# Eight PSUM banks shared out anew in the first expert layer of a graph network with experts

## The chip, the cores and the metric

One core of a Trainium2 chip runs the whole program. The metric is the device time of one execution in microseconds, the median of several runs. The kernel is written by hand in an engine-level language: each engine has its own instruction stream, and all order between engines comes from semaphores.

## The reference

Four layers follow each other on 6250 nodes with 256 features, each added to its input: a graph attention layer over 100000 edges of 8 types, a layer of 32 small experts with one expert a node, a second graph attention layer, and a layer of 8 large experts with two experts a node. The change touches the second of them:

```python
x = x + _L0_ffn_ref(_layernorm(x, axis=-1)[None], router_w, router_b, W1, b1, W2, b2)[0]
# in _L0_ffn_ref, E = 32 experts, D = 256, H = 64
logits = xf @ router_w.T + router_b
idx = jnp.argmax(logits, axis=-1)
h = relu(einsum('nd,ndh->nh', xf, W1[idx]) + b1[idx])
out = relu(einsum('nh,nhd->nd', h, W2[idx]) + b2[idx])
```

## The kernel before

`moe0` (L1374) is that layer. Its first part normalises the 49 tiles of 128 nodes, computes the logits, and sorts the nodes by expert into T = 80 tiles of 128 rows that each belong to one expert (4 more gathers stand at the end of the list and only feed the look-ahead). Its second part, a loop over these tiles in groups of four, is where the change lies. A full group of four is called a round below. For tile n the work is:

- GpSimd gathers the tile's 128 rows from the table of normalised rows, one indirect DMA a tile, into one of 8 slots (L1437). It waits until the slot's last tile has been turned.
- TensorE turns the rows, two 128x128 transposes (`turn`, L1649 to L1655), into 256 columns of a PSUM bank.
- ScalarE copies them out as the high fp16 half (`columns`, L1498 to L1500). VectorE subtracts that from the same PSUM columns and writes the low fp16 half (`column_rest`, L1595 to L1597).
- TensorE makes the inner rows, W1 of the tile's expert times the turned rows, three passes (high by high, high by low, low by high) of two matmuls, 64x128 out (L1660 to L1667).
- ScalarE adds the expert's b1 and applies relu, into `hT` (L1505 to L1507).
- TensorE makes the result, `hT` times W2 of the expert in fp32, 128x256 out (L1671 to L1675). Each appears as two matmul rows in the trace.
- VectorE adds b2 (L1604 to L1607), ScalarE applies relu (L1510 to L1512), and SyncE stores the tile (L1464 to L1466).

The order on each engine is written out by hand. TensorE does, in `four` (L1657): four tiles' inner rows, the turns of the next four, then the four results. ScalarE: four hidden rows, four columns of the next round, four relus. VectorE: four rests of the next round, then four additions. Each engine loads the numbers of the round's experts into registers at its top (`registers`, L282, used in L1504, L1601 and L1659).

A `Count` (L63) is a semaphore that starts at the number of places. `done(eng, t)` waits until tile t is finished. `slot(eng, t)` waits until tile t minus the number of places is finished, which is 4 for `h_ok` and `y_add`.

The eight PSUM banks are paired by tile: tile u of the round has its inner rows in bank 2u, and bank 2u + 1 holds its result in the first 256 columns and the turned rows of the next round in the last 256. Since TensorE may not write a bank while another engine reads it, the result matmul waits, besides for its hidden rows, until VectorE has read the turned rows of the tile in the same bank (L1674), and the turns wait until the additions that read the bank are done (L1669).

Of the kernel before, what the change touches and what calls it, by code (L numbers as in the profile page):

```python
# [8 lines left out]
ALU = mybir.AluOpType  # L9
ACT = mybir.ActivationFunctionType  # L10
AX = mybir.AxisListType

P = 128
N = 6250
D = 256
# [7 lines left out]
E0, F0 = 32, 64  # L23
# [109 lines left out]
def col(ap, start, size=1):  # L133

    out = ap[:, start:start + size] if isinstance(start, int) else ap[:, bass.ds(start, size)]
    if size == 1 and len(ap.shape) > 2:
        names = " ".join("abcd"[: len(ap.shape) - 2])
        out = out.rearrange(f"p o {names} -> p (o {names})")
    return out
# [1234 lines left out]
def moe0(nc, a, k):  # L1374

    with Stage(nc, "moe0") as s:
        bank = s.banks()
# [8 lines left out]
        w1_in, w1 = s.sb("w1_rows", [P, DC, E0, F0]), [s.sb(f"w1_{n}", [P, DC, E0, F0], F16) for n in ("high", "low")]  # L1386
# [13 lines left out]
        xn, xnT = space[:, 0:XN, :], space[:, XN:XN + 2, :]  # L1400
        rw_n, rw = s.sb("router_natural", [E0, D]), s.sb("router", [P, DC, E0])
        rb = s.sb("router_bias", [P, E0])
        w2 = s.sb("w2", [F0, E0, D])
        b1_n, b1, b2 = s.sb("b1_rows", [E0, F0]), s.sb("b1_T", [F0, E0]), s.sb("b2", [P, E0, D])
        x = b2[:, 0:AHEAD * CH, :].rearrange("p (n t) f -> p n t f", n=AHEAD)
# [64 lines left out]
        @block.scalar  # L1470
        def _(act):
            act.dma_start(rw_n[:, :], a["L0_ffn_router_w"]).then_inc(router, 16)
            act.dma_start(rb[:, :], a["L0_ffn_router_b"].rearrange("(o e) -> o e", o=1).broadcast_to([P, E0])).then_inc(router, 16)
            act.dma_start(b1_n[:, :], a["L0_ffn_b1"]).then_inc(router, 16)
            def load_piece(i):
                c, e0 = i % DC, i // DC * EQ
                act.dma_start(w1_in[:, c, e0:e0 + EQ, :], a["L0_ffn_W1"][e0:e0 + EQ, c * P:(c + 1) * P, :].rearrange("e p h -> p e h")).then_inc(loaded, 16)
            for c in range(CHUNKS):
                part = slice(c * CH, (c + 1) * CH)
                act.wait_ge(var_ok, c + 1)  # L1480
                nc.scalar.activation(sd[:, part], var[:, part], ACT.Sqrt).then_inc(sd_ok, 1)
                for t in range(c * CH, (c + 1) * CH):
                    if t >= CH and t % 2 and (t - CH) // 2 < PIECES0:
                        load_piece((t - CH) // 2)
                    if t >= NT - 4:
                        q, h = divmod(t - NT + 4, 2)
                        act.wait_ge(loaded, PIECES0 * 16)
                        nc.scalar.activation(w1[0][:, q, h * E0 // 2:(h + 1) * E0 // 2, :], w1_in[:, q, h * E0 // 2:(h + 1) * E0 // 2, :], ACT.Copy, scale=WS).then_inc(w1_hi, 1)
                    act.wait_ge(t_ps, t + 1)
                    if t >= 2:  # L1490
                        act.wait_ge(lg_ps, t - 1)
                    nc.scalar.activation(xnT[:, t % 2, :], bank[t % 2][:, 0:D], ACT.Copy).then_inc(t_ok, 1)
            route.slot_lanes(act)
            act.wait_ge(route_ok, 1)
            for n in (x_hi, h_ok, y_ok):
                n.start(act)

            def columns(t, u):  # L1498
                x_ps.done(act, t)
                nc.scalar.activation(xT[0][:, u, :], bank[2 * u + 1][:, D:2 * D], ACT.Copy, scale=XS).then_inc(x_hi.sem, 1)  # L1500
            for u in range(4):
                columns(u, u)
            with act.Fori(0, T // 4) as i:
                e = registers(nc, mybir.EngineType.Activation, route.expert[0:1, bass.ds(i * 4, 4)], E0 - 1)  # L1504
                for u in range(4):  # L1505
                    h_ps.done(act, i * 4 + u)
                    nc.scalar.activation(hT[:, u, :], bank[2 * u][0:F0, 0:P], ACT.Relu, bias=col(b1, e[u]), scale=1.0 / (XS * WS)).then_inc(h_ok.sem, 1)  # L1507
                for u in range(4):
                    columns(i * 4 + 4 + u, u)
                for u in range(4):  # L1510
                    y_add.done(act, i * 4 + u)
                    nc.scalar.activation(y[:, u, :], y[:, u, :], ACT.Relu).then_inc(y_ok.sem, 1)  # L1512

        @block.vector
        def _(v):
# [78 lines left out]

            def column_rest(t, u):  # L1595
                x_hi.done(v, t)
                nc.vector.scalar_tensor_tensor(xT[1][:, u, :], bank[2 * u + 1][:, D:2 * D], XS, xT[0][:, u, :], ALU.mult, ALU.subtract).then_inc(x_ok.sem, 1)  # L1597
            for u in range(4):
                column_rest(u, u)
            with v.Fori(0, T // 4) as i:  # L1600
                e = registers(nc, mybir.EngineType.DVE, route.expert[0:1, bass.ds(i * 4, 4)], E0 - 1)  # L1601
                for u in range(4):
                    column_rest(i * 4 + 4 + u, u)
                for u in range(4):  # L1604
                    y_ps.done(v, i * 4 + u)
                    out_ok.slot(v, i, u)
                    nc.vector.tensor_tensor(y[:, u, :], bank[2 * u + 1][:, 0:D], col(b2, e[u]), ALU.add).then_inc(y_add.sem, 1)  # L1607

        @block.tensor
        def _(pe):  # L1610
# [38 lines left out]
            def turn(i, slot):  # L1649

                u = slot % 4
                pe.wait_ge(tile_in[slot], (i + 1) * 16)
                for c in range(DC):
                    last = nc.tensor.transpose(bank[2 * u + 1][:, D + c * P:D + (c + 1) * P], taken(slot)[:, c * P:(c + 1) * P], k.ident[:, :])
                last.then_inc(x_ps.sem, 1)  # L1655

            def four(n, i, half):  # L1657

                e = registers(nc, mybir.EngineType.PE, route.expert[0:1, bass.ds(n, 4)], E0 - 1)  # L1659
                for u in range(4):  # L1660
                    x_ok.done(pe, n + u)
                    h_ok.slot(pe, n + u)
                    for part, (pw, px) in enumerate(passes):
                        for c in range(DC):
                            last = nc.tensor.matmul(bank[2 * u][0:F0, 0:P], col(w1[pw][:, c], e[u]), xT[px][:, u, c * P:(c + 1) * P],
                                                    start=(part == 0 and c == 0), stop=(part == 2 and c == DC - 1))
                    last.then_inc(h_ps.sem, 1)  # L1667
                for u in range(4):
                    y_add.slot(pe, n + u)  # L1669
                    turn(i + half, 4 * (1 - half) + u)  # L1670
                for u in range(4):  # L1671
                    h_ok.done(pe, n + u)

                    x_ok.done(pe, n + 4 + u)  # L1674
                    nc.tensor.matmul(bank[2 * u + 1][:, 0:D], hT[:, u, :], col(w2, e[u]), start=True, stop=True).then_inc(y_ps.sem, 1)  # L1675
            for u in range(4):
                turn(0, u)
            with pe.Fori(0, T // 8) as i:
# [825 lines left out]
```

## Time and profile before

| | us |
|---|---|
| median of 3 runs | 3104.38 (3100.57 to 3109.21) |
| profiled execution, its own time | 3113.99 |
| its span, first to last instruction | 3112.2 |
| mean granted TensorE clock, share of full | 0.781 |
| busy: TensorE matmul, DVE, ACT, GpSimd | 2071.2, 1808.6, 1376.4, 1563.4 |

The tile loop of the first expert layer runs from about 1889 to 2050 us of the span. PE is TensorE's matmul, PEld its weight loads, DVE VectorE, ACT ScalarE, POOL GpSimd. A group row gives starts or counts and busy time, then in brackets the idle time ahead of it and what ended that. In a timeline row, "x4" is four instructions of one line merged: the row's second number is the time from the first one's start to the last one's end. Ends of matmuls are modelled.

### The profile page before, as it was taken

What the parts mean: (1) busy time and instruction counts of PE and PEld (TensorE: products, weight loads), DVE (VectorE), ACT (ScalarE), POOL (GpSimd) and SP (SyncE); (2) the same over time, 40 slices, a digit from 0 to 9 for tenths busy, and PEclk for the clock granted to TensorE, in tenths of its full rate; (3) what the DMA queues carried; (4) which work ended last, traced back from release to release, by engine and by line L of the source; (5) the groups of instructions that cost most, each with busy time, mean ns of one, the idle gap of its engine ahead of it and who ended that gap; (6) DMA issues with size and microseconds to landing.
All of it is one profiled execution on the core that took longest, in us unless ns stands there. A gap on an engine that the chain in (4) does not pass through costs nothing. (4 is left out here: it accounts for less than half of the span.)

```text
span 3112.2 us, 48944 instructions
## 1 busy us (share of the span) xinstructions
PE 2071.2 (67%) x13115; PEld 1560.9 (50%) x13116; DVE 1808.6 (58%) x4427; ACT 1376.4 (44%) x3064; POOL 1563.4 (50%) x1492
## 2 busy tenths in 40 slices
PE   8999216665566555655656546856143599999998
PEld 5555104443344344433444444644032379999997
DVE  5423126565566565665666884445488686656565
ACT  4454125454455444545544124533044664444443
POOL 0066645666666666666662314443640145555554
PEclk9999557687777776777778556768555599999999
DMA  7576533444444444444441623565432162222331
GB/s 232 205 270 257 174 88 113 126 127 117 129 121 121 129 120 123 127 120 119 128 117 33 174 101 92 137 141 144 88 105 65 40 179 47 45 47 46 49 47 27
DMA packets 194692, 363.31 MB, mean 117 GB/s; under 512 B 52783, under 2 KB 127126, under 8 KB 187983
## 3 DMA queue, kind: packets, MB, share of 16 engines
q0 software_dynamic: 78160, 187.31, 25.0%
q1 hardware_dynamic: 106126, 171.10, 16.4%
q10 hardware_dynamic: 10240, 2.95, 0.4%
q8 instruction: 74, 1.21, 0.2%
q14 instruction: 92, 0.75, 0.1%
HBM read 246.22 MB, written 117.28 MB: 117 GB/s over the span
## 5 line engine op out<-in xcount | busy, mean ns | idle before, releaser
L834 POOL DMA_INDIRECT sum_ring<-h_tab,gnn_edge_row x880 | 838.1, 952 | 482.0 <-issue 244.8
L1107 PE MATMUL sum_bank<-sum_ring,sum_one_hot 128*128 128x264 f32 x1760 | 613.2, 494 | 218.0 <-DVE nodes_acc L971 110.8
L1107 PEld LDWEIGHTS sum_bank<-sum_ring,sum_one_hot 128*128 128x128 f32 x1760 | 397.3, 242 | 349.0 <-issue 275.7
L878 ACT ACTIVATE sum_one_hot_T<-sum_distance,sum_pick_unit 128x1024 f16<-128x1024 bf16 x110 | 126.3, 1148 | 619.5 <-remote 569.4
L2235 POOL DMA_INDIRECT out_dram<-moe_y,slots_nodes x112 | 193.4, 1726 | 262.0 <-ACT moe_y L2257 239.9
L964 DVE TENSOR_TENSOR sum_ring<-sum_ring,sum_bank 128x1024 f32<-128x1024 f32 x220 | 266.9, 1214 | 90.4 <-ACT sum_ring L906 85.3
L885 ACT ACTIVATE sum_distance_by_lane<-all_iota,gnn_minus_local 128x128 bf16<-128x128 f32 x880 | 267.4, 386 | 0.1
L2409 PE MATMUL moe_bank<-moe_w_high,slots_early 128*128 x896 | 245.7, 274 | 7.6 <-DVE moe_w_low L1737 7.6
L2409 PE MATMUL moe_bank<-moe_w_high,moe_hidden_low 128*128 x896 | 245.7, 274 | 0.0
L2409 PE MATMUL moe_bank<-moe_w_low,slots_early 128*128 x896 | 245.6, 274 | 0.0
L2226 POOL DMA_INDIRECT moe_tile<-normal,slots_rows x116 | 136.3, 1175 | 187.9 <-PEq L71 134.6
L971 DVE TENSOR_TENSOR nodes_acc<-sum_bank,nodes_acc 128x264 f32 x440 | 187.4, 426 | 39.5 <-remote 24.5
L1096 PE MATMUL sum_bank<-gnn_dst_half_high,sum_one_hot_T 128*128 x880 | 119.2, 215 | 135.8 <-issue 95.1
L2273 ACT ACTIVATE slots_early<-moe_bank,moe_b_T 128x256 f32<-128x256 f32 x456 | 184.6, 478 | 34.9 <-PE moe_bank L2399 19.3
L513 ACT ACTIVATE rows_h_rows<-rows_bank 128x436 f32<-128x436 f32 (+1 forms) x245 | 125.9, 523 | 146.4 <-PE rows_bank L752 126.0
L2399 PE MATMUL moe_bank<-moe_x_high,moe_w_high 128*128 128x256 f16 x912 | 174.5, 273 | 0.4 <-issue 0.4
L2399 PE MATMUL moe_bank<-moe_x_low,moe_w_high 128*128 128x256 f16 x912 | 174.5, 273 | 0.0
L2399 PE MATMUL moe_bank<-moe_x_high,moe_w_low 128*128 128x256 f16 x912 | 174.3, 273 | 0.0
L1096 PEld LDWEIGHTS sum_bank<-gnn_dst_half_high,sum_one_hot_T 128*128 128x128 f16 x880 | 88.3, 111 | 160.2 <-issue 151.7
L942 DVE TENSOR_TENSOR sum_kept_relation<-sum_bank,sum_relation 128x512 f32<-128x512 f32 x110 | 75.5, 686 | 155.4 <-remote 111.0
L2341 DVE SCALAR_TENSOR_TENSOR moe_hidden_low<-slots_early 128x512 f16<-128x512 f32 x228 | 158.3, 694 | 7.8
L752 PE MATMUL rows_bank<-rows_w_high,rows_xnT_high 128*128 128x436 f16 (+1 forms) x490 | 131.6, 350 | 4.6 <-DVE gnn_dst_half_low L626 4.6
(449 smaller groups left out, 4545.6 us busy)
## 6 DMA issues: line engine op xcount, KB each, us to landing
h_tab<-rows_h_rows SPq DMA_DIRECT2D x49, 1056.0 KB
sum_local_rows<-local_tab SPq DMA_DIRECT2D x110, 256.0 KB
slots_stage<-in_L_ffn_W_dram SPq DMA_DIRECT2D x14, 1024.0 KB
sum_ring<-h_tab,gnn_edge_row POOLq DMA_INDIRECT x880
mask_tab<-rows_masks POOLq DMA_DIRECT2D x7, 1560.0 KB
sum_masks<-mask_tab SPq DMA_DIRECT2D x28, 390.0 KB
results<-moe_tiles SPq DMA_DIRECT2D x80, 128.0 KB
g_tab<-gnn_rows_out SPq DMA_DIRECT2D x49, 132.0 KB
```

The lines of the kernel that those rows point to most:

```text
L834: nc.gpsimd.indirect_dma_start(ring[:, t % (RING * ST), :], None, k.h_tab, bass.IndirectOffsetOnAxis(k.edge_row[:, t:t + 1], 0)).then_inc( ...
L885: last = nc.scalar.activation(off[:, u * P:(u + 1) * P], k.iota[:, :], ACT.Abs, bias=k.minus_local[:, m * ST + u:m * ST + u + 1])
L964: nc.vector.tensor_tensor(to, to, by, ALU.mult).then_inc(msg_ok, 1)
L971: nc.vector.tensor_tensor(col(k.acc, b), sum_b[g % SG][:, 0:W0], col(k.acc, b), ALU.add).then_inc(added, 1)
L1096: last = nc.tensor.matmul(pick_b[n % 2][:, u * R * H0:(u + 1) * R * H0], hotT[:, n % 2, u, :], col(part_, b[u // G]), start=(j == 0), stop ...
L1107: last = nc.tensor.matmul(sum_b[j][:, 0:W0], hot[:, m % 3, t, :], ring[:, m % RING * ST + t, :], start=(u == 0), stop=(u == G - 1))
L2226: nc.gpsimd.indirect_dma_start(xi[:, n % 2, h, :], None, k.xn1, bass.IndirectOffsetOnAxis(k.slot_row[:, 2 * n + h:2 * n + h + 1], 0)).then ...
L2235: nc.gpsimd.indirect_dma_start(a["out"], bass.IndirectOffsetOnAxis(k.slot_node[:, 2 * n + h:2 * n + h + 1], 0), y[:, n % 2, h, :], None, b ...
L2273: last = nc.scalar.activation(hg[:, q, m * B1:(m + 1) * B1], bank[q][:, m * B1:(m + 1) * B1], ACT.Gelu, scale=1.0 / (XS * WS), bias=col(b1 ...
L2341: nc.vector.scalar_tensor_tensor(low, f, HS, high, ALU.mult, ALU.subtract).then_inc(hs_ok.sem, 1)
L2399: last = nc.tensor.matmul(bank[q][:, m * B1:(m + 1) * B1], w1[pw][:, c, bass.ds(e * F1 + (2 * q + m) * P, P)], xh[px][:, u, c, :], start=( ...
L2409: last = nc.tensor.matmul(bank[6 + u][:, h * D:(h + 1) * D], hh[ph][:, u, m, h * P:(h + 1) * P], col(w2[pw], e)[:, m * D:(m + 1) * D], sta ...
```

## The change

The turned rows get a bank of their own for each tile (0 to 3), the inner rows two banks in turn (4 and 5), the results two banks in turn (6 and 7). The inner product of tile n now waits until the hidden rows of tile n - 2 have been read out, and the result of tile n until the addition of tile n - 2 has read its bank. The wait of the turns on the additions and the wait of the results on the rests of the next round go.

```diff
+        x_bank, h_bank, y_bank = (lambda u: bank[u]), (lambda u: bank[4 + u % 2]), (lambda u: bank[6 + u % 2])
...
-                nc.scalar.activation(xT[0][:, u, :], bank[2 * u + 1][:, D:2 * D], ACT.Copy, scale=XS).then_inc(x_hi.sem, 1)
+                nc.scalar.activation(xT[0][:, u, :], x_bank(u)[:, 0:D], ACT.Copy, scale=XS).then_inc(x_hi.sem, 1)
...
-                    nc.scalar.activation(hT[:, u, :], bank[2 * u][0:F0, 0:P], ACT.Relu, bias=col(b1, e[u]), scale=1.0 / (XS * WS)).then_inc(h_ok.sem, 1)
+                    nc.scalar.activation(hT[:, u, :], h_bank(u)[0:F0, 0:P], ACT.Relu, bias=col(b1, e[u]), scale=1.0 / (XS * WS)).then_inc(h_ok.sem, 1)
...
-                nc.vector.scalar_tensor_tensor(xT[1][:, u, :], bank[2 * u + 1][:, D:2 * D], XS, xT[0][:, u, :], ALU.mult, ALU.subtract).then_inc(x_ok.sem, 1)
+                nc.vector.scalar_tensor_tensor(xT[1][:, u, :], x_bank(u)[:, 0:D], XS, xT[0][:, u, :], ALU.mult, ALU.subtract).then_inc(x_ok.sem, 1)
...
-                    nc.vector.tensor_tensor(y[:, u, :], bank[2 * u + 1][:, 0:D], col(b2, e[u]), ALU.add).then_inc(y_add.sem, 1)
+                    nc.vector.tensor_tensor(y[:, u, :], y_bank(u)[:, 0:D], col(b2, e[u]), ALU.add).then_inc(y_add.sem, 1)
...
-                    last = nc.tensor.transpose(bank[2 * u + 1][:, D + c * P:D + (c + 1) * P], taken(slot)[:, c * P:(c + 1) * P], k.ident[:, :])
+                    last = nc.tensor.transpose(x_bank(u)[:, c * P:(c + 1) * P], taken(slot)[:, c * P:(c + 1) * P], k.ident[:, :])
...
                     x_ok.done(pe, n + u)
-                    h_ok.slot(pe, n + u)
+                    h_ok.slot(pe, n + u + 2)
...
-                            last = nc.tensor.matmul(bank[2 * u][0:F0, 0:P], col(w1[pw][:, c], e[u]), xT[px][:, u, c * P:(c + 1) * P],
+                            last = nc.tensor.matmul(h_bank(u)[0:F0, 0:P], col(w1[pw][:, c], e[u]), xT[px][:, u, c * P:(c + 1) * P],
...
                 for u in range(4):
-                    y_add.slot(pe, n + u)
                     turn(i + half, 4 * (1 - half) + u)
                 for u in range(4):
                     h_ok.done(pe, n + u)
-
-                    x_ok.done(pe, n + 4 + u)
-                    nc.tensor.matmul(bank[2 * u + 1][:, 0:D], hT[:, u, :], col(w2, e[u]), start=True, stop=True).then_inc(y_ps.sem, 1)
+                    y_add.slot(pe, n + u + 2)
+                    nc.tensor.matmul(y_bank(u)[:, 0:D], hT[:, u, :], col(w2, e[u]), start=True, stop=True).then_inc(y_ps.sem, 1)
```

## Rows read from the trace of the kernel before

**Rows 1.** Busy time by stretch: loop's steady part, three rounds; PEclk is the clock.
```profile
core 0: us, PE busy (x) PEld busy (x) DVE busy (x) ACT busy (x) POOL busy (x), PEclk, DMA share, GB/s
1905.00:2033.00 128.00, 112.29 (x682) 85.87 (x682) 53.73 (x137) 69.70 (x204) 63.98 (x69) 0.77 0.56 138
1963.29:1969.83 6.54, 5.30 (x42) 3.92 (x41) 3.02 (x8) 3.27 (x11) 3.78 (x4) 1.00 0.52 133
1969.83:1977.45 7.62, 6.16 (x41) 4.58 (x41) 3.02 (x8) 4.64 (x15) 3.79 (x4) 0.81 0.55 165
1947.53:1955.83 8.30, 8.30 (x41) 6.59 (x40) 3.40 (x8) 4.60 (x13) 3.77 (x4) 0.50 0.51 151
```

**Rows 2.** Waits in the loop, 1886 to 2052: total us, times, longest.
```profile
POOL moe_tiles L1437 <- PE moe_bank L1654: 26.0, 14, 3.9
POOL moe_pick L1437 <- PE moe_bank L1654: 25.2, 12, 3.8
ACT moe_hidden_T L1507 <- PE moe_bank L1665: 24.2, 25, 3.6
...
PE moe_bank L1675 <- DVE moe_tiles L1597: 7.1, 6, 5.1
...
PE moe_bank L1675 <- issue: 4.9, 7, 0.9
```

**Rows 3.** Timeline of a full-clock round: start, us, engine, line, count, idle before.
```profile
1962.77 0.47 PE L1665 MATMUL moe_bank<-moe_tiles,moe_w_high 128*64 128x128 f16 x4 [0.87 <-issue]
...
1963.29 1.10 PE L1654 MATMUL moe_bank<-all_ident,moe_pick 128*128 128x128 f32 x8
1963.76 1.21 ACT L1500 ACTIVATE moe_tiles<-moe_bank 128x256 f16<-128x256 f32 x4
...
1964.18 1.42 DVE L1597 SCALAR_TENSOR_TENSOR moe_tiles<-moe_bank,moe_tiles 128x256 f16<-128x256 f32 x4 [3.97 <-ACT moe_tiles L1500]
1964.74 1.59 PEld L1675 LDWEIGHTS moe_bank<-moe_w,moe_hidden_T 64*128 64x128 f32 x8 [0.59 <-issue]
1964.75 1.99 PE L1675 MATMUL moe_bank<-moe_w,moe_hidden_T 64*128 x8 [0.36 <-DVE moe_tiles L1597]
...
1965.69 1.61 DVE L1607 TENSOR_TENSOR moe_tiles<-moe_bank,moe_b 128x256 f32<-128x256 f32 x4
1966.14 1.61 ACT L1512 ACTIVATE moe_tiles<-moe_tiles 128x256 f32<-128x256 f32 x4 [1.17 <-DVE moe_tiles L1607]
...
1966.66 0.41 PE L1665 MATMUL moe_bank<-moe_tiles,moe_w_high 128*64 128x128 f16 x4
...
1968.24 0.47 PE L1665 MATMUL moe_bank<-moe_tiles,moe_w_high 128*64 128x128 f16 x4
...
1969.83 1.09 PE L1654 MATMUL moe_bank<-all_ident,moe_tiles 128*128 128x128 f32 x8 [0.54 <-issue]
1969.86 1.12 ACT L1507 ACTIVATE moe_hidden_T<-moe_bank,moe_b_T 64x128 f32<-64x128 f32 x4 [2.11 <-PE moe_bank L1665]
```

**Rows 4.** Timeline of DVE, 1965.9 to 1966.1: additions 0 and 1 merged.
```profile
1965.69 0.76 DVE L1607 TENSOR_TENSOR moe_tiles<-moe_bank,moe_b 128x256 f32<-128x256 f32 x2
```

**Rows 5.** Line L284, the load of expert numbers, on TensorE's sequencer, 1960 to 1970.
```profile
L284 PEldq TENSOR_LOAD <-moe_expert x1: 333/333/333, 1965.9 to 1965.9; - x1
```

**Rows 6.** Timeline of a half-clock round, columns as in rows 3.
```profile
1949.43 3.78 PE L1675 MATMUL moe_bank<-moe_w,moe_hidden_T 64*128 x8
...
1950.89 0.42 DVE L1607 TENSOR_TENSOR moe_tiles<-moe_bank,moe_b 128x256 f32<-128x256 f32 x1 [0.52 <-PE moe_bank L1675]
...
1953.81 0.42 ACT L1512 ACTIVATE moe_tiles<-moe_tiles 128x256 f32<-128x256 f32 x1 [0.44 <-issue]
...
1954.41 0.63 PE L1665 MATMUL moe_bank<-moe_tiles,moe_w_high 128*64 128x128 f16 x4
1954.63 1.12 ACT L1507 ACTIVATE moe_hidden_T<-moe_bank,moe_b_T 64x128 f32<-64x128 f32 x3 [0.41 <-PE moe_bank L1665]
...
1956.03 0.36 ACT L1507 ACTIVATE moe_hidden_T<-moe_bank,moe_b_T 64x128 f32<-64x128 f32 x1 [0.28 <-PE moe_bank L1665]
```

## Prediction

> **What bounds the kernel now.** I read the busy time by stretch first, because the change touches one loop only, the first expert layer's 80 tiles in 20 groups of four; I call one group a round and count its tiles 0 to 3. Nothing of the next layer starts before this loop has ended, so time lost or won there goes one for one into the span. In the steady part TensorE is busy 112.29 of 128 us, DVE 53.73, ACT 69.70 and GpSimd 63.98 [rows 1]: TensorE is the nearest to full, and the granted clock averages 0.77. The single rounds under it show why it is an average: one at clock 1.00 takes 6.54 us from turn to turn with 5.30 us of matmul, the next, partly at the low level, 7.62, and one at 0.50 takes 8.30 us with matmul in all 8.30. So at half clock (1.2 GHz) TensorE is the bound, and at full clock (2.4 GHz) a chain of waits is. Then I read the waits: TensorE's idle time ahead of L1675, where the shared bank makes it wait, is 7.1 us for DVE's L1597 and 4.9 us of issue in the whole stage, and ACT waits 24.2 us for the inner rows of L1665 [rows 2]. GpSimd waits for TensorE, 26.0 and 25.2 us, so the gathers aren't the bound.
>
> Last the order of one full-clock round [rows 3]. Turns start at 1963.29, ACT's columns at 1963.76, DVE's rests at 1964.18; the result matmuls start at 1964.75, the additions at 1965.69, the last relu ends at 1967.75, and the inner products start at 1966.66. ACT's four hidden rows (L1507) come only at 1969.86, 2.11 us after its last relu, though the first inner product is shown ending near 1967.2. At half clock the same step of ACT takes 0.40 us (relu ends 1954.23, hidden row at 1954.63) [rows 6]. So in full-clock rounds some 1.7 us pass in which the release of the inner rows is late; no row says why.
>
> **The change, part by part.** No instruction of work is added or removed; addresses and waits differ.
>
> Removed: TensorE's wait for DVE's rest of the next tile ahead of each result matmul (L1674). It ends a gap of 0.36 us in the round read [rows 3], 12.0 us over the stage at most [rows 2]. The wait on the additions ahead of the turns (L1669) was met long before (additions end at 1967.30, the next turns start at 1969.83): nothing.
>
> Added first: result 2 waits for addition 0, result 3 for addition 1. DVE's program puts all four rests ahead of addition 0, so this doesn't come earlier: addition 0 runs 1965.69 to 1966.11 and addition 1 ends at 1966.45 [rows 3, 4]. A wait that ends reaches the array 0.14 us later (rest 0 ends 1964.60, weights at 1964.74). Result 2 then starts at 1966.25. Eight result matmuls take 1.99 us, so four take about 1.15, and results end at 1967.40 instead of 1966.74: **+0.66 us** for the last addition and relu, which now end at 1968.41. The 0.36 us won at result 0 are lost in this, since results 0 and 1 only finish earlier and stand still. Behind the wait on TensorE's queue stands the load of the next four experts' numbers, now at 1965.9 beside the result matmuls [rows 5]. Inner products start 1.06 us after the last wait (rest 3 ends 1965.60, start 1966.66), so now at 1967.5. That 0.85 us isn't added to the rest, because of the next wait.
>
> Added second: inner product 2 waits for ACT's hidden row 0, and 3 for row 1. Behind it on TensorE are the turns, and who waits for those are ACT, DVE and GpSimd's gathers. If the release is on time, ACT gets to hidden row 0 0.40 us after relu, at 1968.81, takes 0.36 [rows 6], and inner product 2 starts at 1969.31. Product 3 follows by one tile's pitch, (1968.24 - 1966.66) / 3 = 0.53, and the turns 0.52 after it (1962.77 to 1963.29): 1970.36, a round of **7.07 us**. Without the wait the same arithmetic gives 1968.24 + 0.52 = 1968.76, 5.47 us, and the trace shows 6.54 and 7.62, mean 7.08, with the late release.
>
> So a full-clock round has three readings. The late release is in the timed runs of before and goes with the new pause: 7.07 against 7.08, 0.0. It stays in both: 7.07 + 1.7, **+1.7**. It belongs to the recording and is in no timed run: 7.07 against 5.47, **+1.6**. No row shows TensorE pausing between two inner products with a release outstanding, so I take 1.1, nearer to the two that agree, and keep 0.0 and 1.7.
>
> Half-clock rounds: inner product 2 would start at 1954.41; hidden row 0 ends at 1954.63 + 0.36 = 1954.99, plus 0.14: +0.7 us [rows 6]. The result wait costs a little too: addition 0 starts at 1950.89, when result 0 is there, and ends at 1951.31, so result 2 could start at 1951.45; undelayed it would start about half way through the 3.78 us that begin at 1949.43, some 1.85 us in, at 1951.28: **+0.2**, and the relus and hidden row 0 are later by as much. A half-clock round costs **+0.9 us**.
>
> How many: 0.77 is 46% of the time at half level. Of 20 rounds the last has none behind it. Of the other 19, 8 at 8.30 and 11 at 7.08 give 66.4 of 144.3 us at half clock, which is 46%: I take 8 and 11. GpSimd has eight slots and 3.8 us of work in a round, SP's stores follow the relu: both move along, nothing is added.
>
> The sum is 11 x 1.1 + 8 x 0.9 = 12.1 + 7.2 = **+19 us**, with ends 11 x 0 + 7.2 = +7 and 11 x 1.7 + 7.2 = +26. Against the profiled execution (span 3112.2, its own time 3113.99) that is 3133. That execution stands 9.6 us over the median of the runs, 3104.38, which I use: **3123 us**.
>
> Here a rule speaks against the change: the Trainium skill, in Perfetto Trace Analysis, Matmul Optimizations, wants all eight PSUM banks in use so that most instructions can be in flight. Both kernels use eight, but the inner rows drop from four to two; the rows agree in that the pause above is just what the two missing banks cost.
>
> **The rivals.**
> *Covered pause* (the other side, not slower by what can be told): the 1.7 us of late release before inner rows are where the new wait falls, and the pause lets the release come on time. Place: ACT's L1507; price: 0.0 per full-clock round plus at most the 7.2 us, 3104 to 3112 us. It decides if hidden row 0 starts within 0.5 us of the last relu. For it: the release always comes after TensorE's issue gaps late in the inner products. Against: the pause comes at the same place in every round, and the excess of the profiled execution hints that part of the lateness is recording.
>
> *The clock goes down too.* The round at 1.00 has matmul in 5.30 of its 6.54 us, and the round after it already averages 0.81 [rows 1]; with 7.1 to 8.8 us for the same matmuls there is more idle time still. If six of the 11 rounds fell to half clock, each would take 8.30 + 0.9 = 9.2 in place of 7.08 + 1.1 = 8.2: +6 on the sum, 3129 us. If all fell: 11 x (9.2 - 7.08) + 7.2 = +31, 3135 us. Against: at half clock matmul fills the round, and the clock comes back. The Trainium skill's TensorE: Matmul & The Clock Gate, HAM oscillation, has the same: idle TensorE falls to the half rate, and the next work starts at it; the rows agree, with 0.50 and 1.00 inside one stage.
>
> *The shared bank was the cost* (faster): all 12.0 us ahead of the result matmuls go and the new waits are met in time. It decides at addition 0: it would have to end before result 1, at about 1965.3, and ends at 1966.11, since DVE does the rests first. It gives -12.0 + 7.2 = -5; with the half-clock part gone as well -12, which is 3092 to 3099 us. The Trainium skill's PSUM — Partial Sum Buffer, on bank collisions, is the rule behind it: guard by bank and not by address, so that own banks need no guard between rests and results.
>
> That the change doesn't do what it says isn't likely: the three bank functions name eight different banks, and each has its wait.
>
> **How the numbers follow.** What a measurement of this kernel can tell from no change is about 0.3%, 9.3 us. The forecast (+9.3 to +26, 3114 to 3130) gets 0.55, the clock rival 0.15, the covered pause 0.22, the shared bank 0.08. Slower is the first two, 0.70; same 0.22; faster 0.08. The range takes in the whole covered pause, from 3104, and the clock rival at its top, 3135, with the 4 us by which runs of before lie off their median: 3104 to 3140.
>
> **What would show it.** Right: in full-clock rounds a gap on TensorE of 0.5 us or more ahead of the third inner product, ended by ACT's L1507; one ahead of the third result matmul, ended by DVE's L1607; none ended by L1597; L1507 in two pairs rather than four in a row; a turn-to-turn time of 7.1 us or more at full clock and 9.2 at half. Wrong: hidden row 0 starting within 0.5 us of relu while rounds stay at 7.1, which is the covered pause; rounds below 6.5 us, which is the shared bank; a mean clock below 0.7 in the stage, which is the clock rival.

## The result and the profile after

The changed kernel's median is 3141.97 us (3133.09 to 3145.71, 4 runs) against 3106.8 us (3100.57 to 3110.1, 4 runs) for the kernel before, run beside it: **ratio 1.0096, 95% interval 1.0075 to 1.0118**. Slower, by about 30 us of 3107. The ratio on record is not the quotient of the two medians, which is 1.0113, or 35 us; I go by the ratio. It was measured a second time (after_again, below): 1.0107, interval 1.0085 to 1.013. Of the versions below, one run of own (4867.52 us) and one of after_act (4213.99 us) lie far above all others and are in no ratio.

I read the profiled execution in the same order as before. First the busy time by stretch. These are the head of the page of the changed kernel and its granted clock in 40 slices:

```profile
span 3137.0 us, 48924 instructions
...
PE 2103.7 (67%) x13115; PEld 1577.8 (50%) x13116; DVE 1808.4 (58%) x4427; ACT 1386.4 (44%) x3064; POOL 1564.3 (50%) x1492
...
PEclk9999558777787677877688555559555599999999
```

The same lines of the kernel before:

```profile
span 3112.2 us, 48944 instructions
...
PE 2071.2 (67%) x13115; PEld 1560.9 (50%) x13116; DVE 1808.6 (58%) x4427; ACT 1376.4 (44%) x3064; POOL 1563.4 (50%) x1492
...
PEclk9999557687777776777778556768555599999999
```

The number of matmuls is the same, 13115, and TensorE is busy 32.5 us longer with them. DVE and GpSimd do the same work in the same time. Nothing was added, so the matmuls themselves ran slower: the clock. In the slices (some 78 us each) the loop lies in the 25th to 27th: 555 after, 676 before. The windows tell it exactly. Busy time by stretch, kernel after (columns as in rows 1): the whole loop from the first turn to the end of the last relu, two rounds that follow each other, and the stretches behind the loop:

```profile
1886.00:2083.10 197.10, 173.89 (x808) 122.14 (x808) 68.49 (x164) 91.83 (x244) 77.22 (x82) 0.54 0.42 107
1936.15:1945.78 9.63, 8.95 (x41) 6.28 (x40) 3.39 (x8) 4.54 (x12) 3.77 (x4) 0.50 0.35 109
...
1945.78:1954.14 8.36, 7.20 (x41) 5.38 (x40) 3.20 (x8) 4.51 (x12) 3.77 (x4) 0.70 0.40 106
...
2083.10:2286.00 202.90, 81.99 (x354) 63.99 (x354) 101.41 (x331) 45.58 (x125) 108.97 (x112) 0.68 0.51 124
```

and the kernel before:

```profile
1889.30:2048.50 159.20, 132.61 (x808) 100.33 (x808) 64.46 (x164) 82.95 (x244) 77.11 (x82) 0.76 0.54 131
...
2048.50:2260.00 211.50, 83.33 (x354) 64.64 (x354) 101.51 (x330) 45.09 (x125) 111.26 (x115) 0.67 0.50 122
```

The loop takes 197.1 us in place of 159.2, **+37.9 us**, with the same 808 matmuls, and the mean granted clock falls from 0.76 to 0.54. There is no round at the full level in this execution. Of the 18 rounds that follow the fill of the pipe, 13 take 9.60 to 9.63 us at 0.50 (the row at 1936.15 is one), four 8.32 to 8.39 us at about 0.70 (the row at 1945.78) and one 8.95 us; in the kernel before they take 5.49 to 8.31 us (three of them in [rows 1]), 7.38 on average against 9.30 now. That is 18 x 1.92 = 34.6 us; the other 3.3 us are at the two ends of the loop.

The spans differ by 24.8 us only. The stretch ahead of the loop was 3.3 us shorter in this execution (1886.0 against 1889.3), and the time behind the loop 9.8 us shorter (3137.0 - 2083.1 = 1053.9 against 3112.2 - 2048.5 = 1063.7), most of it in the stretch next to the loop, 202.9 against 211.5 us for the same 354 matmuls. The change doesn't touch either. Behind the loop it is the profiled execution of the kernel before that stands out, with its 1063.7 us: in the two executions of the changed kernel and the eight of the versions below that leave the stages behind the loop alone this time is 1047.8 to 1057.8 us, and its whole time was 9.6 us over its median as well. So the two spans understate the change, and the ratio of the timed runs (+30 us) stands between span and loop. From here on I compare loops.

Second the waits. Waits of TensorE in the loop, 1886 to 2084, kernel after (total us, times, longest):

```profile
PE moe_bank L1655 <- DMA moe_tiles<-normal,moe_slot_rows: 12.4, 4, 10.8
PE moe_bank L1666 <- ACT moe_hidden_T L1508: 8.9, 15, 1.2
PE moe_bank L1674 <- DVE moe_tiles L1608: 5.0, 6, 2.5
PE moe_bank L1666 <- issue: 4.8, 7, 2.5
```

The wait on DVE's rests that stood here before (L1597, 7.1 us) [rows 2] is gone. In its place are the two new ones, 8.9 us ahead of the inner products (L1666) for ACT's hidden rows (L1508) and 5.0 us ahead of the results (L1674) for DVE's additions (L1608). The first row is the fill of the pipe at the start, 10.8 us in one piece. In the second execution the two waits are 11.2 and 6.4 us. The 8.9 us is no large number against 37.9: the waits give the place, not the price.

Third a half-clock round of the kernel after, the timeline (columns as in rows 3):

```profile
1936.15 1.97 PE L1655 MATMUL moe_bank<-all_ident,moe_pick 128*128 128x128 f32 x8
...
1938.05 4.21 PE L1674 MATMUL moe_bank<-moe_w,moe_hidden_T 64*128 x8
...
1939.52 0.42 DVE L1608 TENSOR_TENSOR moe_tiles<-moe_bank,moe_b 128x256 f32<-128x256 f32 x1 [0.52 <-PE moe_bank L1674]
...
1940.18 0.50 PEld L1674 LDWEIGHTS moe_bank<-moe_w,moe_hidden_T 64*128 64x128 f32 x2 [0.78 <-issue]
...
1942.19 0.63 PE L1666 MATMUL moe_bank<-moe_tiles,moe_w_high 128*64 128x128 f16 x4
...
1942.83 0.63 PE L1666 MATMUL moe_bank<-moe_tiles,moe_w_high 128*64 128x128 f16 x4
1942.86 0.42 ACT L1513 ACTIVATE moe_tiles<-moe_tiles 128x256 f32<-128x256 f32 x1 [0.44 <-DVE moe_tiles L1608]
...
1943.68 0.62 ACT L1508 ACTIVATE moe_hidden_T<-moe_bank,moe_b_T 64x128 f32<-64x128 f32 x2 [0.41 <-PE moe_bank L1666]
...
1944.29 0.64 PE L1666 MATMUL moe_bank<-moe_tiles,moe_w_high 128*64 128x128 f16 x4 [0.62 <-ACT moe_hidden_T L1508]
...
1945.78 1.54 PE L1655 MATMUL moe_bank<-all_ident,moe_tiles 128*128 128x128 f32 x6
```

The reader is to see two things. The eight result matmuls take 4.21 us, where they took 3.78 [rows 6]: result 2 waits for addition 0, which starts at 1939.52 and ends at 1939.94, and the weights come at 1940.18. And the third inner product, which would follow the second by its pitch of 0.64 us at 1942.83 + 0.64 = 1943.47, starts at 1944.29, because ACT's hidden row 0 starts at 1943.68, 0.41 us after its last relu. That is +0.43 and +0.82 us; the rest of the +1.33 us (9.63 - 8.30), 0.08 us, lies between the third product and the turns.

### The profile page after: what moved, and what is told of

The parts are those of the page before. It is cut to its first block and busy times, and to the rows that moved or that the text cites. A ratio compares the mean times of both kernels' runs of the same rounds, so it can differ in the third digit from the quotient of the medians.

```text
span 3137.0 us, 48924 instructions
## 1 busy us (share of the span) xinstructions
PE 2103.7 (67%) x13115; PEld 1577.8 (50%) x13116; DVE 1808.4 (58%) x4427; ACT 1386.4 (44%) x3064; POOL 1564.3 (50%) x1492
## 3 DMA queue, kind: packets, MB, share of 16 engines
q0 software_dynamic: 78160, 187.31, 24.8%
## 5 line engine op out<-in xcount | busy, mean ns | idle before, releaser
L977 DVE TENSOR_SCALAR sum_under_max<-sum_bank 128x256 f32<-128x256 f32 x28 | 11.9, 424 | 214.0 <-remote 213.3
```

## The experiments

Loop times are from the first turn to the end of the last relu in one profiled execution of each; two executions of the changed kernel have 197.1 and 192.6 us, so a few us are scatter. Ratios are those on record, to the kernel before run beside each; where they are set against each other, remember their intervals of some 0.002 to each side (6 us). The granted clock is that of the loop.

| kernel | ratio (95%) | loop, us | clock |
|---|---|---|---|
| before | 1 | 159.2 | 0.76 |
| after | 1.0096 (1.0075 to 1.0118) | 197.1 | 0.54 |
| after_again | 1.0107 (1.0085 to 1.013) | 192.6 | 0.58 |
| own | 0.9977 (0.9961 to 0.9994) | 149.2 | 0.80 |
| h2 | 1.0068 (1.0042 to 1.0095) | 180.0 | 0.67 |
| y2 | 1.0016 (0.9996 to 1.0036) | 164.0 | 0.79 |
| fill | 1.005 (1.0032 to 1.0068) | 171.5 | 0.87 |
| before_fill | 0.9989 (0.9979 to 1.0) | 157.3 | 0.84 |
| own_fill | 0.9981 (0.9968 to 0.9994) | 146.0 | 0.91 |
| after_act | 1.0084 (1.0061 to 1.0107) | 181.6 | 0.65 |
| after_both | 1.0082 (1.0066 to 1.0099) | 182.2 | 0.66 |
| nostore | 1.0117 (1.0088 to 1.0145), stores behind the loop | 161.1 | 0.73 |

Own, h2, y2 and fill ran on one chip; the other fills and orders on a second, and on that one nostore and after_again later, together.

### own: no wait between tiles u and u + 2

The turned rows keep a bank each. The inner row and the result of one tile share a bank, in different columns: the result of tile n is written only when its hidden row has been read, so their lives don't overlap.

```diff
-        x_bank, h_bank, y_bank = (lambda u: bank[u]), (lambda u: bank[4 + u % 2]), (lambda u: bank[6 + u % 2])
+        x_bank, h_bank, y_bank = (lambda u: bank[u]), (lambda u: bank[4 + u]), (lambda u: bank[4 + u][:, D:2 * D])
...
-                    h_ok.slot(pe, n + u + 2)
+                    y_add.slot(pe, n + u)
...
-                    y_add.slot(pe, n + u + 2)
```

> Turned rows in banks 0 to 3 as in the change, but inner rows and result of a tile share bank 4 + u, so that neither new wait stands: the result matmul waits for its own hidden rows alone, the inner product for the addition of tile n - 4. Theory (the two new waits cost the time, directly and through the clock): no loss against the kernel before, a loop of 135 us or less between the first result and the last, ratio 0.990 to 1.000. Rival (it is the new place of the turned rows, or some effect of bank addresses): as slow as the changed kernel, ratio about 1.010.

Measured: 3079.82 us against 3085.31, ratio 0.9977 (0.9961 to 0.9994), the loop 149.2 us; from the first result to the last it is 138.0 us, a little over the 135 expected. The loop and a full-clock round of own in the windows:

```profile
1870.80:2020.00 149.20, 127.67 (x808) 96.43 (x808) 60.85 (x164) 79.57 (x244) 77.13 (x82) 0.80 0.59 140
...
1903.58:1909.51 5.93, 5.31 (x41) 3.96 (x41) 2.74 (x8) 3.60 (x12) 3.78 (x4) 1.00 0.54 161
...
1943.08:1951.39 8.31, 8.31 (x42) 6.60 (x41) 3.37 (x8) 4.92 (x14) 3.78 (x4) 0.50 0.54 162
```

The half-clock round is back at 8.31 us, with matmul in all of it, as in the kernel before [rows 1]. Own is 7 us faster than the kernel before by the ratio, 10 by the loop. That is most likely the removed wait on the rests, though own also gives inner row and result one bank, and no run takes the two apart. What costs in the change is the two banks in turn, not the new places of the turned rows. This version beats both kernels, the kernel before by a little. Its late release is still there: in the round about 1897 of own ACT stands

```profile
1897.25 1.12 ACT L1508 ACTIVATE moe_hidden_T<-moe_bank,moe_b_T 64x128 f32<-64x128 f32 x4 [2.17 <-PE moe_bank L1666]
```

2.17 us ahead of its four hidden rows. No inner product waits for them here; the first to read them are the results, behind the turns, and what these wait is small over the whole loop:

```profile
PE moe_bank L1673 <- ACT moe_hidden_T L1508: 3.3, 5, 2.1
```

### h2 and y2: each of the two pairs by itself

h2 is the kernel before with the inner rows in two banks in turn:

```diff
-                    nc.scalar.activation(hT[:, u, :], bank[2 * u][0:F0, 0:P], ACT.Relu, bias=col(b1, e[u]), scale=1.0 / (XS * WS)).then_inc(h_ok.sem, 1)
+                    nc.scalar.activation(hT[:, u, :], bank[2 * (u % 2)][0:F0, 0:P], ACT.Relu, bias=col(b1, e[u]), scale=1.0 / (XS * WS)).then_inc(h_ok.sem, 1)
...
-                    h_ok.slot(pe, n + u)
+                    h_ok.slot(pe, n + u + 2)
...
-                            last = nc.tensor.matmul(bank[2 * u][0:F0, 0:P], col(w1[pw][:, c], e[u]), xT[px][:, u, c * P:(c + 1) * P],
+                            last = nc.tensor.matmul(bank[2 * (u % 2)][0:F0, 0:P], col(w1[pw][:, c], e[u]), xT[px][:, u, c * P:(c + 1) * P],
```

> The kernel before with the inner rows alone moved to two banks in turn, so that only the wait of an inner product for the hidden row of tile n - 2 is added. Theory (this wait is the larger one, +0.7 of the +0.9 us in a half-clock round, and it is enough to keep the clock low): rounds of about 9 us, ratio 1.006 to 1.010, mean clock of the loop below 0.65. Rival (the wait of the results is the one that matters): ratio below 1.004 and a loop clock near the 0.77 of before.

y2 is own with the results in two banks in turn:

```diff
-        x_bank, h_bank, y_bank = (lambda u: bank[u]), (lambda u: bank[4 + u]), (lambda u: bank[4 + u][:, D:2 * D])
+        x_bank, h_bank, y_bank = (lambda u: bank[u]), (lambda u: bank[4 + u]), (lambda u: bank[6 + u % 2][:, D:2 * D])
...
+                    if u < 2:
+                        h_ok.done(pe, n + u + 2)
+                    y_add.slot(pe, n + u + 2)
```

Since its results lie in the banks of inner rows 2 and 3, results 0 and 1 wait for those hidden rows too. That binds once, while the pipe fills (5.1 us, with the first two rounds 1.7 us longer than in own), and in no steady round.

> Turned rows in banks 0 to 3, inner rows in banks 4 to 7, results in two banks in turn (columns 256 to 511 of banks 6 and 7), so that only the wait of a result for the addition of tile n - 2 binds. Theory (the hidden-row wait is the larger part): full-clock rounds longer by up to 0.8 us, half-clock rounds by 0.2, ratio 1.001 to 1.005. Rival (this wait is what lowers the clock): ratio 1.008 or more, loop clock below 0.65.

Measured: h2 1.0068 (3111.13 against 3085.31 us), loop 180.0 us; y2 1.0016 (3091.44), loop 164.0. Busy time of the loop of h2, and its wait rows:

```profile
1882.10:2062.10 180.00, 146.41 (x808) 110.40 (x808) 66.64 (x164) 89.02 (x244) 77.50 (x82) 0.67 0.47 116
```

```profile
PE moe_bank L1665 <- ACT moe_hidden_T L1507: 14.1, 18, 2.5
```

The wait for hidden rows alone is seen 18 times and costs 180.0 - 159.2 = 20.8 us of loop, 21 us by the ratio; the half-clock round is 9.15 to 9.18 us, +0.9. The clock, 0.67, did not fall below the 0.65 expected. In y2 the wait stands ahead of the third result, here in a full-clock round:

```profile
1909.05 1.09 PE L1655 MATMUL moe_bank<-all_ident,moe_tiles 128*128 128x128 f32 x8
...
1911.93 1.12 PE L1676 MATMUL moe_bank<-moe_w,moe_hidden_T 64*128 x4 [0.74 <-DVE moe_tiles L1608]
```

The wait costs 164.0 - 149.2 = 14.8 us of loop against own, and (1.0016 - 0.9977) x 3085 = 12 us by the ratios. The prediction left out the later start of the inner products (0.85 us), as covered by the wait for hidden rows. Alone the result wait is worth 0.4 us in a half-clock round (8.73 against 8.31) and brings full-clock rounds to 7.0 to 7.3 us. Both together, after against own, are 47.9 us of loop (43.4 with the second execution), 12.3 (7.8) more than the sum of the two. By the ratios the two add up to 0.0107 and both together are 0.0119 (0.0130 with after_again), a difference within the intervals: that they cost more together than apart is seen in the profiled loops and not shown by the timed runs. The clock goes the same way as the loops: 0.80 (own), 0.79 (y2), 0.67 (h2), 0.54 (both).

### fill, before_fill, own_fill: the same waits at another clock

Ten small matmuls, whose result nobody reads, are put into the pause ahead of the third inner product, where TensorE would otherwise stand still:

```diff
+                    if u == 2:
+                        for _ in range(10):
+                            nc.tensor.matmul(bank[0][0:F0, D:D + P], w1[0][:, 0, 0, :], xT[0][:, 0, 0:P], start=True, stop=True)
```

fill adds them to the changed kernel, own_fill to own; in before_fill they go to the idle columns of bank 1, behind a wait for the addition that last read it.

> The changed kernel with ten extra 64x128 matmuls into unused columns of bank 0 between the second and the third inner product of a round, work that the reference doesn't have and nothing reads. At full clock they take about 0.6 us, at half clock 1.1 us, in the place of the new wait. Theory (idle time in the wait keeps the clock at half): the clock rises in more of the loop, above 0.65 from 0.55, and the kernel is no slower than the changed one or up to 15 us faster. Rival (the waits cost time by themselves and the clock follows from something else): clock stays at 0.55, and the kernel is as slow or slower by up to 20 x 0.3 = 6 us.

> The kernel before with the same ten extra matmuls, into unused columns of bank 1, between the second and the third inner product; nothing reads them. At full clock they add about 0.6 us to a round, at half clock 1.1. Theory (the clock follows how busy TensorE is kept, and half-clock rounds are the dear ones): the loop's mean clock rises from 0.77 to above 0.85, and the loop's time stays within 5 us of the 159 us before in spite of 200 more matmuls. Rival (the clock doesn't follow them): clock 0.77, the loop longer by 19 x 0.6 to 19 x 1.1 = 11 to 21 us.

> The kernel without either wait (turned rows in banks 0 to 3, inner rows and result of a tile in bank 4 + u) with the ten extra matmuls into bank 0. Loop so far 149.3 us at a clock of 0.81. Theory of the clock: nearly all rounds at full clock, mean above 0.88, rounds of 6.5 to 7.3 us, so the loop at 140 to 150 us and the kernel level with the one without them. Rival: clock stays at 0.81, the loop 11 to 20 us longer.

The loop of fill, and one of its rounds:

```profile
1872.80:2044.30 171.50, 136.35 (x1008) 101.61 (x1008) 60.30 (x164) 84.22 (x244) 77.18 (x82) 0.87 0.50 123
...
1951.47:1959.18 7.71, 6.10 (x52) 4.42 (x51) 2.93 (x8) 4.13 (x12) 3.79 (x4) 1.00 0.53 142
```

With 200 matmuls more than the changed kernel (1008 against 808) the loop is 25.6 us **shorter** (171.5 against 197.1), TensorE's busy time 37.5 us shorter (136.35 against 173.89), and the clock is 0.87 in place of 0.54. The ratio goes from 1.0096 to 1.005, the intervals apart. So with the clock come back 25.6 of 37.9 us by the loops, and 0.0046 of 0.0096, 14 of 30 us, by the ratios; the other 171.5 - 159.2 = 12.3 us of loop stay. The round of fill shows the longer chain of waits at full clock:

```profile
1954.35 1.12 PE L1677 MATMUL moe_bank<-moe_w,moe_hidden_T 64*128 x4 [0.74 <-DVE moe_tiles L1608]
...
1956.60 0.72 PE L1664 MATMUL moe_bank<-moe_tiles,moe_w_high 128*64 128x128 f16 x10
...
1957.08 0.36 ACT L1508 ACTIVATE moe_hidden_T<-moe_bank,moe_b_T 64x128 f32<-64x128 f32 x1 [0.58 <-issue]
...
1957.68 0.47 PE L1669 MATMUL moe_bank<-moe_tiles,moe_w_high 128*64 128x128 f16 x4 [0.36 <-ACT moe_hidden_T L1508]
...
1958.66 0.47 PE L1669 MATMUL moe_bank<-moe_tiles,moe_w_high 128*64 128x128 f16 x4 [0.40 <-ACT moe_hidden_T L1508]
```

The ten (0.72 us, L1664) lie in the pause; it is still not filled, 0.36 us are left, and the fourth product has a wait of its own, 0.40 us.

On the others the same ten do little: before_fill 0.9989 with 157.3 us, clock 0.84 (just under the 0.85 expected); own_fill 0.9981 with 146.0 us, clock 0.91, against own's 0.9977 and 149.2 us. The loop of before_fill:

```profile
1874.50:2031.80 157.30, 128.00 (x1008) 102.28 (x1008) 62.41 (x164) 80.80 (x244) 77.47 (x82) 0.84 0.57 134
```

In own_fill 13 of the 18 rounds are at 1.00 and still take 5.4 to 7.6 us: there a chain of waits bounds the round, and a higher clock has little left to give.

The pair fill and before_fill also gives a fairer price of the waits, since both have the ten: 1.0050 - 0.9989 = 0.0061, 19 us, or 171.5 - 157.3 = 14.2 us of loop. Of the loss without them that leaves 11 us by the ratios and 23.7 us by the loops to what goes with the low clock. So the clock's part is a third to a half by the timed runs and over 60% by the profiled loops; the rest is the two waits themselves. A reading that fits is that the changed kernel's clock stays down because its rounds at half clock have a pause in them as well. That the small matmuls raise the clock is shown by the three; that nothing else of them works is not.

### after_act and after_both: another order on ACT and DVE

If the price is that ACT does all four relus ahead of hidden row 0, hidden rows first should take it away. after_act:

```diff
                 for u in range(4):
+                    if u == 1 and not first:
+                        for w in (2, 3):
+                            relu(i * 4 - 4 + w, w)
...
-                for u in range(4):
-                    y_add.done(act, i * 4 + u)
-                    nc.scalar.activation(y[:, u, :], y[:, u, :], ACT.Relu).then_inc(y_ok.sem, 1)
+                for u in range(2):
+                    relu(i * 4 + u, u)
```

(the lines of the first loop follow the hidden row of u; the first round is peeled, and the last two relus stand behind the loop). after_both has DVE's additions between the rests as well:

```diff
-                for u in range(4):
-                    column_rest(i * 4 + 4 + u, u)
-                for u in range(4):
+                for op, u in ((0, 0), (0, 1), (1, 0), (0, 2), (1, 1), (0, 3), (1, 2), (1, 3)):
+                    if op == 0:
+                        column_rest(i * 4 + 4 + u, u)
+                        continue
```

> The changed kernel with ScalarE's order altered: hidden rows 0 and 1 of a round come ahead of relus 2 and 3 of the round before. Banks and waits are those of the change. Theory (the third inner product waits because ScalarE's hidden row 0 stands behind the last relu and the register load): the gap ahead of the third inner product shrinks from 0.62 us to 0.1 or less, the kernel comes to where the results' wait alone stands, ratio 1.001 to 1.004 instead of 1.010. Rival (the two banks are too few whatever ScalarE's order): ratio 1.008 or more.

> As the last, and VectorE's order altered too: rest 0, rest 1, addition 0, rest 2, addition 1, rest 3, additions 2 and 3, so that result 2 doesn't wait for all four rests. Theory: both new waits nearly vanish with the banks of the change kept; ratio 0.996 to 1.001, loop 150 to 160 us. Rival (the rests are now late for the next inner products, or the banks themselves cost): ratio 1.004 or more.

Both miss, and the rivals' ratios, 1.008 or more and 1.004 or more, are met. The ratios are 1.0084 and 1.0082 (26 and 25 us), within the interval of the changed kernel; the loops, 181.6 and 182.2 us, are 22 and 23 us over the kernel before, and shorter than the 197.1 and 192.6 us of the changed kernel's two executions. So the order buys back a part at most, and no part that the timed runs can show. Here is the round of after_both at the higher clock:

```profile
1958.29 1.35 PE L1686 MATMUL moe_bank<-moe_w,moe_hidden_T 64*128 x4 [0.49 <-DVE moe_tiles L1620]
...
1962.24 0.36 ACT L1512 ACTIVATE moe_hidden_T<-moe_bank,moe_b_T 64x128 f32<-64x128 f32 x1 [1.40 <-PE moe_bank L1678]
...
1962.85 0.65 PE L1678 MATMUL moe_bank<-moe_tiles,moe_w_high 128*64 128x128 f16 x4 [1.12 <-ACT moe_hidden_T L1512]
```

The fourth product waits for hidden row 1, which ACT starts at 1962.24, after 1.40 us idle, though the records of its inner product (the second) end at 1961.04. That is the late release of the prediction. In own little waits for it (3.3 us in all); with two banks in turn TensorE itself waits for it, 1.12 us here. At half clock the order helps (rounds of 9.2 instead of 9.6 us). So an earlier place for the hidden rows buys back 0.4 us in some rounds, and is exposed to the release in others.

### nostore: is the late release the stores'?

In the kernel before, the loop's stores of the results are left out and 80 stores of the same size come after the loop; so the rows that are stored are not the layer's, and its time outside the loop is not to be compared.

```diff
-                sp.dma_start(rows(k.ys0, (i * 4 + u) * P, P), y[:, u, :]).then_inc(out_ok.sems[u], 16)
+                sp.sem_inc(out_ok.sems[u], 16)
...
+            for t in range(T):
+                sp.dma_start(rows(k.ys0, t * P, P), y[:, t % 4, :]).then_inc(late_st, 16)
+            sp.wait_ge(late_st, T * 16)
```

> The kernel before with SyncE's 80 stores of result tiles taken out of the loop (the semaphore is counted up in their place) and issued after it, so that the rows stored are the last four tiles' and not the layer's; some 60 us of stores stand behind the loop. It asks where ScalarE's late hidden rows of full-clock rounds come from (2.1 us after the last relu instead of 0.4). Theory A (SyncE's store issues hold up TensorE's releases): the gap falls to about 0.4 to 0.6 us in all rounds and full-clock rounds take 5.5 to 6.5 us. Theory B (it comes from the dense inner products alone): the gap stays near 2 us in full-clock rounds.

Measured: a loop of 161.1 us against 159.2, with half the traffic:

```profile
1881.50:2042.60 161.10, 136.88 (x808) 103.62 (x808) 65.07 (x164) 84.85 (x244) 77.23 (x82) 0.73 0.33 68
```

68 GB/s instead of 131, and nothing gained. Three of its rounds still have ACT stand 2.07 to 2.16 us between relu and hidden row; others above half clock have mostly 0.66 to 1.58 us. One of each:

```profile
1925.87 1.18 ACT L1511 ACTIVATE moe_hidden_T<-moe_bank,moe_b_T 64x128 f32<-64x128 f32 x4 [2.09 <-PE moe_bank L1669]
...
1931.63 0.36 ACT L1511 ACTIVATE moe_hidden_T<-moe_bank,moe_b_T 64x128 f32<-64x128 f32 x1 [0.68 <-PE moe_bank L1669]
```

The stores don't bound the loop. They may have a part in the lateness: in the four rounds at 0.97 to 1.00 the first hidden row comes 0.66 to 1.34 us after the last relu, where such rounds of the kernel before have 1.68 to 2.12 us in all but the last, but the second hidden row then waits another 0.53 to 1.27 us. They aren't the only cause. What the cause is stays open.

### after_again

The changed kernel once more, no edit, beside nostore.

> The changed kernel once more, beside the same runs of the kernel before as the others of this set. Theory: a ratio of 1.008 to 1.012, the loop at 190 to 198 us and its clock near 0.55. Rival (the low clock of the first profile was one execution's chance): clock above 0.65 and a loop below 185 us.

Measured: 3137.51 against 3104.54 us, 1.0107 (1.0085 to 1.013). The loop takes 192.6 us at 0.58, with rounds of 9.63 us at 0.50 in 12 of the 18; two rounds are at 0.90 and 0.91 and take 7.79 and 8.25 us. The low clock is the kernel's, not one execution's.

## Why the prediction was right, and where it was not

**The side** was right, and by its mechanism: the wait of inner product 2 on ACT's hidden row 0. Undoing the two pairs (own) takes the whole loss away, and h2 alone gives 21 us of it. But it is not the whole mechanism: the rival *the clock goes down too*, which also makes the kernel slower and had got 0.15, is at work beside it. **The number** is short. Forecast 3123 us, +19; measured 3141.97 us, which is 2 us above the upper end of the range, 3140. Part of that is the kernel before, whose median rose from 3104.38 to 3106.8 us; by the ratio, 3104.38 x 1.0096 = 3134 us, +30, the time of the rival *the clock goes down too*, all rounds (3135 us). Step by step:

- **Removed wait (taken at nothing).** The row of L1597 is gone, but it was most likely worth more than nothing: own, without it and without the waits on tile n - 2, gains 7 us. With the result wait added the gain is gone, as forecast (y2, 1.0016).
- **Result wait at full clock (+0.66 us).** Placed right. In fill result 2 starts 2.88 us after the turns (1954.35 - 1951.47), forecast 1966.25 - 1963.29 = 2.96.
- **Inner product 2 at full clock.** Forecast 6.02 us after the turns (1969.31 - 1963.29), in fill 6.21 (1957.68 - 1951.47). The failed piece is "Product 3 follows by one tile's pitch": it was put 0.53 us behind product 2 and stands 0.98 behind it, since its own wait for hidden row 1 (0.40 us) is a second link. So the round is 7.71 us and not 7.07.
- **The three readings.** The first one's premise holds in the profiled executions: the pause takes the place of the late release. In fill ACT's gap ahead of hidden row 0 is 0.58 us, and in the changed kernel 0.40 to 0.61 us in 17 of the 18 rounds, against up to 2.17 us before. But its 0.0 didn't follow, for the reason above: 7.71 against 7.08 is +0.6 (the ten matmuls lie in the pause and add nothing to it as long as 0.36 us of it are left). I had taken +1.1, the mean of the three; the size lies between. In the changed kernel's first execution no round is at full clock, so this term carried nothing of its loop's 37.9 us.
- **Half-clock rounds (+0.9 us).** Mis-sized: +1.33. Result wait +0.43 for +0.2: from the end of addition 0 to the weights it is 1940.18 - 1939.94 = 0.24 us, where 0.14 had been taken from full clock, and result 2 would by these rows have started about 1.70 us in (3.78 less the 2.08 us from 1940.18 to the end), not 1.85. Hidden row +0.82 for +0.7, again by 0.25 us for 0.14 (1943.68 + 0.36 = 1944.04 to 1944.29). h2, which has only the second, shows +0.9.
- **How many rounds (8 at half clock, 11 at full).** This is the step that failed, and by the profile it carries most of the difference. 13 of 18 were at 0.50, none at 1.00. The prediction's argument against the clock rival was: "at half clock matmul fills the round, and the clock comes back". It holds for the kernel before, 8.30 of 8.30 us [rows 1]. The forecast itself had put 0.9 us of waiting into that round and so taken its own ground away: in the changed kernel matmul is in 8.95 of 9.63 us, the wait is inside the half-clock round as well, and the next is at 0.50 again. I counted the price of a wait at each level and left the number of rounds at each as it had been. The fills show the size: 23.7 to 25.6 us of the 37.9, or 11 to 14 of 30 by the ratios.
- **The signs.** Half-clock rounds of 9.2 us and more, TensorE's gaps ended by L1508 and L1608 (the numbers of L1507 and L1607 after the change), none ended by the rests, hidden rows in pairs (x2 at 1943.68): all seen, though at half clock and at 0.70, since there was no round at full clock to see them in. A mean clock below 0.7 in the stage is seen too (0.54 and 0.58), and that was set down as a sign of being wrong, the clock rival's.
- **The other rivals.** Covered pause: the release came on time, as it says, the rounds didn't stay at 7.1. Shared bank: no round is below 6.5 us, and own (-7 us) suggests that what is right in it, a price of the removed wait, is real, and comes only without the pairs.

The new waits in the list are 8.9 and 5.0 us, the loop is 37.9 us longer, and 25.6 us of that come back with the clock at 0.87. In the Trainium skill, TensorE: Matmul & The Clock Gate, A second HAM failure mode: psum-queue depth-cycling, a kernel that cycles through PSUM banks each iteration has small idle times between groups of matmuls, often enough that the clock goes back and forth, and its throughput suffers. The trace agrees that small waits and the clock go together, but not in the form: the changed kernel's clock mostly stays down, 0.50 in 13 of 18 rounds, and it is the kernel before that goes back and forth between 0.50 and 1.00 [rows 1].

## What to carry to other kernels

Two banks in turn put the other engine's whole answer (its queue, its work, the signal back) on TensorE's path in each round; count the engine's place in its own order before giving a buffer only two copies, and count every tile's wait, not the first alone. Here banks were better shared between things of one tile whose lives follow each other, inner row and result, which beat both kernels at 0.9977. And where TensorE's clock changes inside a stage, a new pause can have two prices, its length and the rounds that then stay at the low level: ask of each level whether the pause is in it too.

## What was not expected of the hardware

- Matmul records cover 8.95 of 9.63 us in a round (93%), and the granted clock stays at 0.50, round after round (13 of 18). Ten more small matmuls in each round bring 0.87. Rounds of the kernel before with matmul in all 8.31 us at 0.50 are followed by rounds at 0.83 to 0.89. What in the changed kernel's rounds keeps the clock down, the 0.7 us without matmul or where they lie, no run here tells.
- After bursts of inner products at or near full clock ACT gets to the hidden rows of the kernel before 1.6 to 2.2 us after its last relu, though TensorE's records of the first product end long before; at half clock it takes 0.41 us. The full clock alone isn't enough: the last round of the kernel before (1.00) and the last four of own_fill (0.84 to 1.00) have 0.41 us. It stays without the stores in part (2.07 to 2.16 us in three rounds), and when the new pause follows the second product it is gone (0.4 to 0.6 us). It isn't an artefact without price: in after_both TensorE waits 1.12 us for it. Whether the timed executions have it in the same size was not tried.
